# The second attention's query tiles taken large beside small, in place of in order of size

## What is computed

```python
scores = jnp.einsum('bhsd,bhtd->bhst', q, k) / math.sqrt(float(DH))
mask = jnp.tril(jnp.ones((S, S), dtype=scores.dtype))
scores = scores * mask
scores = jnp.where(scores == 0.0, -jnp.inf, scores)
attn = jax.nn.softmax(scores, axis=-1)
out = jnp.einsum('bhst,bhtd->bhsd', attn, v)
```

## Time and profile before

| | |
|---|---|
| median of 3 runs | 1240.81 us (1238.11 to 1241.08) |
| the profiled execution | 1239.13 us |
| its span, first to last instruction | 1237.3 us |
| second attention, first to last mask | about 748 to 1171 us |
| mean granted PE clock | 0.958 of full |

### The profile page before, as it was taken

One profiled execution on the slowest core, in us unless ns is written; L12 is line 12 of the kernel. 1 busy time (PEld: TensorE's weight loads), 2 busy tenths in 40 slices (PEclk: granted clock), 3 DMA queues, 4 the chain that ended last, 5 costly groups with the idle time before them and its releaser, 6 DMA issues.

```text
span 1237.3 us, 28186 instructions
## 1 busy us (share of the span) xinstructions
PE 1121.1 (91%) x10202; PEld 851.2 (69%) x10202; DVE 862.2 (70%) x2486; ACT 815.4 (66%) x1915; POOL 349.4 (28%) x345
## 2 busy tenths in 40 slices
PE   5999999999999999999899976987888888888886
PEld 3787878787888787888576653665566556556674
DVE  6656566565656565645334547999999899999863
ACT  3766666767666666631233434998889889989932
POOL 1974646455464646213001202000000000000043
PEclk8999999999999999999599995998999899999998
DMA  6222223222322323211011043020310202110001
GB/s 161 59 69 76 69 58 77 63 59 64 80 54 70 76 59 75 65 36 34 15 35 43 25 97 46 2 40 27 66 31 10 40 6 36 26 15 2 2 1 34
DMA packets 33627, 58.90 MB, mean 48 GB/s; under 512 B 4906, under 2 KB 18114, under 8 KB 33490
## 3 DMA queue, kind: packets, MB, share of 16 engines
q1 hardware_dynamic: 32690, 55.52, 19.9%
q10 hardware_dynamic: 800, 1.57, 0.4%
HBM read 27.59 MB, written 4.33 MB: 26 GB/s over the span
## 4 chain that ended last, share of the span: by engine, by line
PE 56%; DVE 18%; issue 11%; ACT 7%; POOL 5%; DMA 2%; SPq 1%; ACTq 0%; POOLq 0%; DVEq 0%
PE pT L1278 12%; PE pO L1201 12%; PE pS L1239 10%; DVE Zb L956 9%; PE pS L1352 4%; ACT probs L719 3%; PE pT L1149 3%; PE pT L1365 3%; DVE Sm L971 3%; PE pS L1313 2%; PE pT L1153 2%; PE pS L1430 1%; ACT PT L699 1%; PE pS L1410 1%; DMA KS<-split 1%
## 5 line engine op out<-in xcount | busy, mean ns | idle before, releaser
L1278 PE MATMUL pT<-cst,probs 128*128 128x128 f32 x2304 | 369.9, 287 | 53.4 <-ACT probs L719 49.2
L1278 PEld LDWEIGHTS pT<-cst,probs 128*128 128x128 f32 x2304 | 257.0, 143 | 149.0 <-ACT probs L719 99.7
L719 ACT ACTIVATE probs<-probs,nmax 128x128 f32<-128x128 f32 (+7 forms) x256 | 198.7, 776 | 129.9 <-DVE nmax L966 128.9
L699 ACT COPY PT<-pT 128x512 f32<-128x512 f32 (+3 forms) x576 | 263.9, 482 | 16.8 <-PE pT L1278 15.6
L966 DVE CUSTOM_DVE_ANT_0 probs<-pS,causal_wide 128x128 f32<-128x128 f32 (+7 forms) x256 | 192.0, 750 | 91.2 <-PE pS L1239 83.6
L719 ACT ACTIVATE probs<-Sm,nmax 128x128 f32<-128x128 f32 (+7 forms) x256 | 199.6, 780 | 55.4 <-DVE nmax L971 49.1
L1201 PE MATMUL pO<-PT,V 128*64 128x128 f32 (+1 forms) x4608 | 233.5, 281 | 2.5 <-DVE attnT L925 1.1
L956 DVE TENSOR_SCALAR Zb<-pS 128x128 bf16<-128x128 f32 (+7 forms) x256 | 192.7, 753 | 20.0 <-PE pS L1245 19.4
L1201 PEld LDWEIGHTS pO<-PT,V 128*64 128x64 f32 (+1 forms) x4608 | 180.9, 114 | 36.3 <-issue 21.0
L971 DVE CUSTOM_DVE_ANT_0 Sm<-pS,Zb 128x128 f32<-128x128 f32 (+7 forms) x256 | 193.3, 755 | 4.5
L543 POOL TENSOR_TENSOR rstd<-rstd,power 128x4 f32<-128x4 f32 x32 | 32.6, 1019 | 552.4 <-DVE rstd L824 552.4
(11 more groups left out here) (189 smaller groups left out, 1370.2 us busy)
## 6 DMA issues: line engine op xcount, KB each, us to landing
wq_t<-factors SPq DMA_DIRECT2D x32, 256.0 KB, 4.0
Qs<-Ql SPq DMA_DIRECT2D x30, 256.0 KB, 3.7
Kh<-Kh SPq DMA_DIRECT2D x30, 256.0 KB, 3.4
Kl<-Kl SPq DMA_DIRECT2D x30, 256.0 KB, 4.6
QS<-split SPq DMA_DIRECT2D x72, 64.0 KB
KS<-split SPq DMA_DIRECT2D x72, 64.0 KB
w1s<-in_w SPq DMA_DIRECT2D x16, 128.0 KB, 2.3
w2s<-in_w SPq DMA_DIRECT2D x16, 128.0 KB, 2.2
```

Of the source, the lines that this page charges most:

```text
L699: nc.scalar.copy(PT[:, g % 2, h, k0 * P:(k0 + nk) * P], pT[r % TBANKS][:, 0:nk * P])\
L719: nc.scalar.activation(probs[:, i % NPROB, 0:n], src[:, 0:n], ACT.Exp, bias=nmax[:, i % 4:i % 4 + 1], scale=-1.0, accum_out=total).then_in ...
L1278: m = nc.tensor.transpose(pT[r % TBANKS][:, kt * P:(kt + 1) * P], probs[:, item % NPROB, (k0 + kt) * P:(k0 + kt + 1) * P], ident)
```

## The change

The order of the tiles of the second attention becomes 0, 7, 1, 6, 2, 5, 3, 4 in the even halves and the same backwards, 4, 3, 5, 2, 6, 1, 7, 0, in the odd ones. The first attention (two heads in a group) keeps its order. Everything else is the same program text.

```diff
         self.heads = heads
-        tiles = list(range(ST)) if heads > 2 else [t + h * (ST // 2) for t in range(ST // 2) for h in range(2)]
+        tiles = [t if h == 0 else ST - 1 - t for t in range(ST // 2) for h in range(2)] if heads > 2 else [t + h * (ST // 2) for t in range(ST // 2) for h in range(2)]
         order = [(0, qt) for qt in tiles] + [(1, qt) for qt in reversed(tiles)]
```

## The result

The new order took 1286.76 us (median of 4 runs, 1285.81 to 1287.29) against 1239.46 us before (4 runs): 1.0381 times, 95% interval 1.0362 to 1.0400. The profiled execution took 1286.6 us. In a later comparison on another chip the same kernel came to 1286.44 us, 1.0378 times (1.0332 to 1.0424).

What follows compares the result with a forecast made beforehand. DVE was taken to bound the second attention. The profiled 1239.1 + 41 (pairs two to four) + 8 (first pair) + 10 (PE's clock) = 1298.1, with 1.7 for the median 1300 us; range 1272 to 1330.

Steps and rivals of the forecast that it cites:

- The bound: DVE bounds the second attention; its 16.3 us of idle time is the most an order can win.
- The chain: Small tile behind large: large exponential, two items' copies, small exponential, values, a remainder; pairs two to four +41 us.
- the rest: Remainder of a small tile's time after exponentials, copies and values: 0.88 us, plus 0.5 before tiles 5 to 7.
- The first pair: First two halves, which have side work by step number: 14.8 − 6.5 + 3 − 3, +8 us, bounds 0 and 15.
- the side work: In the first two halves, DVE's extra work hides 6.5 us of loss; ACT's extra copies add about +3.
- The clock: PE's clock falls at every second of 24 rises: 12 × 1.2 = 14, less 1 + 3 from old halves, +10 us.
- dear case: A fall of PE's clock that doubles the values of tile 7 in the chain: 1.9 us.
- the clock holds: Rival: PE's gaps stay too short for a fall of its clock; 1286 us, chance 0.25.
- looser chain: Rival: values do not bind the next tile's scores, only two steps per boundary are slow; 1261 us, chance 0.10.
- no effect: Rival: DVE stays fed everywhere and losses of falling halves only change places; 1241 us, chance 0.03.
- a gain: Rival: large tiles' surplus PE and ACT work fills small tiles' time; 1224.5 us at best, 1232 by half, chance 0.04.

Runs made afterwards that it cites:

- the clock experiment: New order plus four useless 512-column PE matmuls in the second to fourth item of each tile larger than the one before: 1290.7 us (1.0412).
- the second profile: The new order unchanged, run and profiled again on the chip of the kernel with added matmuls: 1286.4 us (1.0378 of the kernel before).

## Why it came out so

**The forecast** of 1300 us, with a range from 1272 to 1330, was 13 us too high.

**The bound** was read right. DVE's work stayed within 4 us, and its idle time rose from 15.9 to 56.6 us in the stage (about 70 had been forecast). No order without waits could have won more than the 15.9.

**The chain** was read right, down to its parts. ACT and PE in the new seventh half, from tile 7's last maximum to tile 6's first mask, answer to the earlier trace rows:

```profile
1121.47 0.42 DVE L956 TENSOR_SCALAR Zb<-pS 128x256 bf16<-128x256 f32 x1
...
1121.65 1.15 ACT L719 ACTIVATE probs<-Sm,nmax 128x1024 f32<-128x1024 f32 x1
...
1122.80 1.05 ACT L699 COPY PT<-pT 128x512 f32<-128x512 f32 x2
...
1122.94 1.13 PE L1278 MATMUL pT<-cst,probs 128*128 128x128 f32 x8 [0.94 <-ACT probs L719]
...
1123.74 0.51 ACT L719 ACTIVATE probs<-Sm,nmax 128x256 f32<-128x256 f32 x1
...
1124.24 1.07 ACT L699 COPY PT<-pT 128x512 f32<-128x512 f32 x2
...
1125.36 1.93 PE L1201 MATMUL pO<-PT,V 128*8 128x128 f32 x64 [0.24 <-ACT PT L699]
...
1127.50 0.54 PE L1239 MATMUL pS<-KS,QS 72*128 72x512 bf16 x2
...
1128.14 1.09 DVE L956 TENSOR_SCALAR Zb<-pS 128x896 bf16<-128x896 f32 x1 [2.17 <-PE pS L1245]
```

The exponential of tile 7's last item (1121.65), the copies of the item before (1122.80), the small exponential (1123.74), its own copies (1124.24), the values (1125.36, 0.24 idle on that copy), the scores (1127.50) and the mask (1128.14, 2.17 idle) follow each other as the prediction listed them. Each boundary came out 0.15 to 0.4 us shorter than worked out, save those from 5 to 3 and from 4 to 3:

| boundary | worked out | measured (sixth, seventh half) |
|---|---|---|
| 7 to 1 | 7.07 | 6.67 |
| 6 to 2 | 6.66 | 6.29 |
| 5 to 3 | 6.05 | 6.14 |
| 4 to 3 | 5.55 | 5.79 |
| 5 to 2 | 6.14 | 5.88 |
| 6 to 1 | 6.55 | 6.26 |
| 7 to 0 | 6.47 | 6.32 |

With the filling of the clock experiment, at the full clock, 6 to 1 took 6.18 and 7 to 0 6.13; the other five are within 0.02 of the table.

The sum of the mis-sized parts for 7 to 1 is plain in the rows: what I called the rest, taken from a small boundary, was 1.38 and is 1.08 (0.18 ahead of the exponential, 0.05 ahead of the values, 0.85 behind them), and the first pair of copies holds ACT for 0.94 and not 1.05. The rises cost nothing, as said (tile 7 9.82, tile 6 8.76). The three later pairs were to cost 41 us over the old order, without any clock. They cost 33.9, with 3.5 us of falls of the clock in the old fourth and fifth half gone from the comparison (0.8 of tile 7, 2.7 of tiles 1 and 2), so 37.4; less the 1.0 us of the new falls, 36.4.

**The first pair** was forecast at +8 and measured at +10.5 in one profile and +12.0 in another. Of the +10.5, 1.5 belong to no boundary. In the second half PE sat idle for 3.87 us at the start of tile 5, and the profile names nothing that it waited for:

```profile
833.39 0.47 PE L1278 MATMUL pT<-cst,probs 128*128 128x128 f32 x1 [3.87 <-issue]
```

The tile took 11.42 us, and 9.95 in the second profile, where PE idled 1.25 us at this place. The cause of the longer idle time is open. Without the 1.5 the first pair is +9.0, and the second profile gives the same: +11.6, of which 2.5 are the falls in tiles 2, 1 and 0. The +9.0 is close to the forecast, but by two errors that offset one another. A pair without side work costs 12.1 (36.4 / 3) and not 13.8, and the side work took 3.1 off that and not 5.8. Which of its terms was off was not tried.

**The clock** is the step that failed: the term 12 × 1.2. The count was about right. The trace's clock record has eleven falls for the 21 rises of the last six halves, fifteen in the second profile, and four more in the first two halves of each (the stage has 28 rises, not the 24 that the prediction counted). The price was not. It was put at 1.2 us a fall and is 0.1 to 0.25 in the mean of the last six halves. The eleven and the fifteen all begin in a large tile, 5, 6 or 7, that follows a small one, and there PE has time to spare even at the lower level; by the next boundary the clock is mostly back. The prediction's dear case, a fall over the values of a large tile in the chain, is real (1.4 us, measured above; it was put at up to 1.9), but it came in the first pair alone and never in the last six halves. The old fourth half's fall, from which the lower bound of 0.8 came, sat in a tile 7 with another large tile before it, and the one of the old fifth half, at 2.7, in tiles 1 and 2; PE probably had less slack there, which was not tried. So in this kernel the clock's net effect on the last six halves is near −2.5 to 0 us and not +10 for the stage.

The forecast for the profiled run, 1298.1, was 11.5 us above its 1286.6: 3.6 by the later pairs' chain (41 against 37.4) and 13.5 by the clock (+10 against −3.5, the new falls being already in the 37.4), less 2.5 for the first pair and 3.1 for the time outside the stage, which differs from run to run. The rival "the clock holds" gave 1286 and hit the time, in part by luck: it had 3.6 us too much for the chain and 5.6 too little for the first pair and the time outside the stage. Its mechanism is not what happened either. The clock fell, with PE idle for 1.93 us at the longest ahead of a fall, and in the last six halves it hardly mattered. The rule of the Trainium skill that the prediction cites ("TensorE: Matmul & The Clock Gate", "HAM oscillation — how this bites in real kernels") asks for longer gaps than that; here the measurement decides. The rivals of a looser chain, of no effect and of a gain fall by the rows above: the masks behind a boundary wait.

## What to carry to other kernels

Engines that lag each other by a few items are balanced only while neighbouring items are of a size. An engine that is second by little (ACT at 48 of DVE's 48.5 us a half) turns into the limit wherever large work still passes through it while the bound engine already has small work, and the bound engine never gets that time back. Sort by size and meet at equal sizes; before interleaving, price one large-to-small boundary by the chain from the last large item's first result to the next buffer, and multiply. And a fall of PE's clock is to be priced by the slack that PE has in the tile where it falls: 0.1 to 0.25 us in the mean in large tiles here, 1.4 where it met the values of a large tile in a small one.

## What was not expected of the hardware

The clock fell with PE idle only for short times just before: 1.93 us was the longest ahead of any fall in the last six halves of the two profiles, 1.11 ahead of the one shown above, and 0.79 ahead of three falls in tile 5 of the second profile. It was granted in full in these six halves when four more matmuls were put into such waits. Eleven and fifteen falls cost little there: 334.0 us at 0.92 and 336.4 at 0.90, against 333.0 at 1.00.
